# Four raw buffers for the first-layer expert weights, asked for four groups ahead

## What is computed

```python
def _moe_forward(x, router_w, router_b, w1, b1, w2, b2, top_k=2):
    logits = einsum('bsd,de->bse', x, router_w) + router_b
    top_vals, top_idx = top_k(logits, 2)
    keep = one_hot(top_idx, E).sum(-2) > 0
    gating = softmax(where(keep, logits, -1e30))
    h = relu(einsum('td,edh->eth', xf, w1) + b1[:, None, :])   # w1: 8 x 512 x 2048
    y = einsum('eth,ehd->etd', h, w2) + b2[:, None, :]         # w2: 8 x 2048 x 512
    out = einsum('etd,te->td', y, gf)
```

## Time and profile before

| | us |
|---|---|
| median of 3 runs | 1210.54 (1209.79 to 1211.63) |
| the profiled execution | 1207.57 |
| its span | 1205.8 |
| busy in the span: PE / DVE / ACT / POOL | 1102.9 / 926.9 / 694.9 / 474.2 |

### The profile page before, as it was taken

The page is one execution under the profiler, slowest core; times in us unless marked ns, Lnnn a source line. Parts: engine busy times, 40 slices in busy tenths (PEclk is TensorE's granted clock), DMA queues, the critical chain, the costliest instruction groups (busy, mean ns, idle before and its releaser), DMA issues.

```text
span 1205.8 us, 22592 instructions
## 1 busy us (share of the span) xinstructions
PE 1102.9 (91%) x7196; PEld 1014.9 (84%) x7197; DVE 926.9 (77%) x2049; ACT 694.9 (58%) x1387; POOL 474.2 (39%) x416
## 2 busy tenths in 40 slices
PE   4899999999999999999999999767887999788995
PEld 4799999999999999999999999644666987667895
DVE  6578888988888888889888888876776565876554
ACT  3456566565565665655656656441566665655654
POOL 6355656656556556556556552000121011121011
PEclk9899999999999999999999999975999999899998
DMA  5221121121221221211211210422777656776663
GB/s 182 96 73 57 47 71 42 59 71 39 62 71 39 62 59 50 62 52 58 62 51 59 62 42 2 152 105 59 256 244 233 206 173 231 233 247 193 199 191 96
DMA packets 78320, 131.11 MB, mean 109 GB/s; under 512 B 11336, under 2 KB 36040, under 8 KB 78288
## 3 DMA queue, kind: packets, MB, share of 16 engines
q1 hardware_dynamic: 74272, 120.73, 30.9%
q0 software_dynamic: 4016, 9.96, 3.7%
HBM read 123.34 MB, written 7.34 MB: 108 GB/s over the span
## 4 chain that ended last, share of the span: by engine, by line
PE 74%; DVE 11%; issue 5%; ACT 4%; DMA 3%; DVEq 1%; POOL 0%; ACTq 0%; SPq 0%; POOLq 0%
PE ps L421 17%; PE ps L423 16%; PE ps L422 16%; PE ps L1372 7%; PE ps L1424 7%; PE ps L1408 4%; PE ps L1409 3%; DMA w_raw<-in_w_dram 2%; DVE w_lo L1081 2%; DVE w_lo L1089 2%; DVE mx L1017 1%; DVE k_mix L939 1%; DVE pt_mix L1031 1%; ACT probs L749 1%; PE ps L1384 1%
## 5 line engine op out<-in xcount | busy, mean ns | idle before, releaser
L562 POOL TENSOR_TENSOR ctx_hi<-ctx_raw,no_query 128x1152 fp32r<-128x1152 f32 x64 | 143.0, 2234 | 290.5 <-PE ps L423 281.5
L939 DVE SCALAR_TENSOR_TENSOR k_mix<-ps,bk_sb,k_mix 64x384 fp32r<-64x384 f32 (+1 forms) x256 | 162.3, 634 | 82.2 <-ACT k_mix L709 77.9
L749 ACT ACTIVATE probs<-ps,negmax 128x1152 f32<-128x1152 f32 x64 | 78.3, 1223 | 200.9 <-DVE negmax L1020 200.9
L421 PE MATMUL ps<-wv_hi,ctx_hi 128*128 128x256 f32 (+1 forms) x624 | 181.9, 291 | 6.7 <-DVE k_mix L939 6.5
L566 POOL TENSOR_TENSOR ctx_lo<-ctx_raw,ctx_hi 128x1152 fp32r<-128x1152 f32 x64 | 179.7, 2807 | 5.0
L423 PE MATMUL ps<-wv_hi,ctx_lo 128*128 128x256 f32 (+1 forms) x624 | 175.8, 282 | 0.0
L422 PE MATMUL ps<-wv_lo,ctx_hi 128*128 128x256 f32 (+1 forms) x624 | 175.0, 280 | 0.0
L709 ACT ACTIVATE k_mix<-ps,bk_sb 64x384 fp32r<-64x384 f32 (+1 forms) x256 | 150.8, 589 | 24.1 <-PE ps L423 19.6
L1031 DVE TENSOR_TENSOR pt_mix<-ps,pt_mix 128x384 fp32r<-128x384 f32 (+1 forms) x256 | 142.1, 579 | 1.4 <-ACT pt_mix L760 1.4
L421 PE MATMUL ps<-ctx_hi,wk_hi 128*128 128x384 f32 (+1 forms) x384 | 133.4, 347 | 0.0
L423 PE MATMUL ps<-ctx_hi,wk_lo 128*128 128x384 f32 (+1 forms) x384 | 132.3, 345 | 0.0
(11 more groups left out here) (216 smaller groups left out, 2565.4 us busy)
## 6 DMA issues: line engine op xcount, KB each, us to landing
w_raw<-in_w_dram SPq DMA_DIRECT2D x68, 1024.0 KB, 6.8
ctx_raw<-in_ctx_t_dram SPq DMA_DIRECT2D x48, 576.0 KB, 3.8
ctx_raw<-in_ctx_t_dram SPq DMA_DIRECT2D x16, 673.5 KB, 4.0
q_both<-q_scratch SPq DMA_DIRECT2D x14, 128.0 KB, 3.0
x<-in_x_dram SPq DMA_DIRECT2D x1, 1024.0 KB, 5.5
wq_raw<-in_wq_dram SPq DMA_DIRECT2D x1, 1024.0 KB, 7.8
q_scratch<-q_out SPq DMA_DIRECT2D x1, 1024.0 KB, 5.8
wo_raw<-in_wo_dram SPq DMA_DIRECT2D x1, 1024.0 KB, 5.1
```

What stands on the lines that cost most here:

```text
L421: pe.matmul(acc_ap, a_hi, b_hi, start=start, stop=False)
L562: nc.gpsimd.tensor_tensor(ctx_hi[slot][:, :, 0:n], ctx_raw[slot][:, :, 0:n], no_query[:].rearrange("p (o i) -> p o i", o=1).broadcast_to([ ...
L939: last = nc.vector.scalar_tensor_tensor(out=k_mix[other, 2 * a + i, cols], in0=ps[rows, bank, 0:m], scalar=bk_sb[rows, a:a + 1], in1=k_mix ...
```

## The change

w1's raw pieces get two more buffers, `w1_more`, in the region that the output projection's weights leave (12 rows of 512 values; 8 of them are taken). The helper `w1_raw(group)` names the buffer of a group modulo 4, and each buffer has its own semaphore. Ahead of the loop, SP waits until the output projection has been multiplied (`x1_product`), then loads w1 of groups 2 and 3 of expert 0, and only then waits for the normalised rows and stores them. In the loop, at the place where SP loaded w1 of group `g + 2`, it now loads w1 of group `g` of the next block. The high and low parts keep two slots, and w2 keeps its two raw slots and its place in the order. At the end POOL waits for four w1 semaphores. Two more 1 MB loads are made in all.

```diff
+        w1_more = place("w1_more", [P, HG - 2, 4, BANK], F32, moe)
-        place("stage2_rest", [P, 3 * KD - BT, D], F32, moe)
+        place("stage2_rest", [P, 3 * KD - BT - 4 * (HG - 2), D], F32, moe)
-        w1_loaded = [sem(f"w1_loaded{i}") for i in range(2)]
+        w1_loaded = [sem(f"w1_loaded{i}") for i in range(HG)]
+        def w1_raw(group):
+            slot = group % HG
+            return w_raw[slot][:, 0] if slot < 2 else w1_more[:, slot - 2]
...
-                sp.dma_start(w_raw[slot][:, 0], src).then_inc(w1_loaded[slot], 16)
+                sp.dma_start(w1_raw(g), src).then_inc(w1_loaded[g], 16)
...
+            sp.wait_ge(x1_product, TT)
+            for g in range(2, HG):
+                load_w1(0, g)
             sp.wait_ge(xn_ready, 2 * TT)
...
                     sp.wait_ge(w1_split, pieces_done(b, g, PIECES - 1))
-                    load_w1(owner_next, (g + 2) % HG, g % 2)
+                    load_w1(expert_next, g)
                     sp.wait_ge(w2_split, pieces_done(b, g, PIECES - 1))
                     load_w2(owner_next, (g + 2) % HG, g % 2)
...
-                    act.wait_ge(w1_loaded[slot], 16 * (HG // 2 * b + group // 2 + 1))
-                nc.scalar.copy(w_hi[slot][:, 0, piece_of(piece), :], w_raw[slot][:, 0, piece_of(piece), :]
+                    act.wait_ge(w1_loaded[group % HG], 16 * (b + group // HG + 1))
+                nc.scalar.copy(w_hi[slot][:, 0, piece_of(piece), :], w1_raw(group)[:, piece_of(piece), :]
```

More of the change, by code:

```diff
@@ L493, in _, with load_w1 @@
             w2_view = w2.rearrange("e (g j p) d -> e g p j d", p=P, j=4)
-            def load_w1(e, g, slot):
+            def load_w1(e, g):
                 cols = slice(g * BANK, (g + 1) * BANK)
@@ L504, in load_w2 @@
                 sp.dma_start(w_raw[slot][:, 1], src).then_inc(w2_loaded[slot], 16)
-            load_w1(0, 0, 0)
+            load_w1(0, 0)
             load_w2(0, 0, 0)
             sp.wait_ge(pv_taken, STEPS * B + 1)
-            load_w1(0, 1, 1)
+            load_w1(0, 1)
             load_w2(0, 1, 1)
+            sp.wait_ge(x1_product, TT)
+            for g in range(2, HG):
+                load_w1(0, g)
             sp.wait_ge(xn_ready, 2 * TT)
@@ L678, in _ @@
             for i in range(2):
-                pool.wait_ge(w1_loaded[i], 16 * (HG // 2 * blocks + 1))
                 pool.wait_ge(w2_loaded[i], 16 * (HG // 2 * blocks + 1))
+            for i in range(HG):
+                pool.wait_ge(w1_loaded[i], 16 * (blocks + 1))
             pool.wait_ge(rows_moved, all_moved)
@@ L1080, in w1_low_piece @@
                 dve.wait_ge(w1_high, pieces_done(b, group, piece))
-                nc.vector.tensor_tensor(w_lo[slot][:, 0, piece_of(piece), :], w_raw[slot][:, 0, piece_of(piece), :],
+                nc.vector.tensor_tensor(w_lo[slot][:, 0, piece_of(piece), :], w1_raw(group)[:, piece_of(piece), :],
                                         w_hi[slot][:, 0, piece_of(piece), :].bitcast(F32),
```

## The result

| | before | after |
|---|---|---|
| median, us | 1210.16 (1207.86 to 1211.63, 4 runs) | 1194.62 (1192.12 to 1195.65, 4 runs) |
| ratio, 95% interval | | 0.9866 [0.9844, 0.9889] |
| the profiled execution / its span | 1207.57 / 1205.8 | 1195.65 / 1193.9 |

A forecast was written before the change was run, and what follows sets the result against it. VectorE was taken to carry the narrow blocks, idling behind ScalarE's wait for late w1. Removing that gives 14.7 us, less 2.0 for TensorE's clock: 12.7 us off the 1210.5 us median, 1197.8 us, range 1193.5 to 1203.

The forecast's parts named there:

- The late w1 and its price: Narrow blocks, groups 2 and 3: VectorE's idling behind ScalarE's wait for w1 goes, a gain of 14.7 us.
- w2 does not take its place: Narrow blocks: tightest w2 lands in about 5 us, under the 9.4 us limit, no cost; rival 1204.2 us, chance 0.07.
- The additions ahead of the loop: Two more w1 loads after the output projection cost nothing; rival of a late store, about 1213 us at worst, chance 0.04.
- What carries the block then: Narrow block after the change: VectorE stays the longest at 6.4 us per group, 0.3 us over TensorE.
- The DMA share of a narrow block: Same loads in 33 to 34 us instead of 37.9: the share goes from 0.77 to about 0.87.
- The clock: TensorE at block changes: half-speed falls cost 3.7 us, less 1.7 lost today, so 2.0 us to pay.
- the forecast's own range: Total time 1195.5 to 1200 us, for 0 to 3.5 clock falls, chance 0.70.
- the clock comes back: Rival: no block change is followed by a TensorE clock fall, 16.4 us gained, 1194.1 us; chance 0.08.
- no fall: Lower bound of the clock term at block changes: without any fall TensorE gives back 1.7 us.
- half-speed stretches at the starts of blocks: Sign of being right: after the change TensorE's half-speed stretches stand at block starts.
- the wide range: Total time 1193.5 to 1203 us, taking in both clock cases and leaving out the last three rivals.
- The rule on oscillation: Trainium skill: TensorE's clock stays up once waits for transfers are gone, turning the 2.0 us cost into 1.7 us gained.

The follow-up runs named there:

- two-ahead kernel: Changed kernel with its four buffers, but w1 asked for two groups ahead again and no extra loads ahead of the loop: 1210.69 us, ratio 1.0001.
- e_after_again: The changed kernel itself, unaltered, measured on another occasion: 1193.20 us, ratio 0.9875.
- w2 second in the queue: Changed kernel with both waits of a group first, then both loads, w1 ahead of w2: 1193.49 us, ratio 0.9879.
- three ahead: Changed kernel with w1 asked for three groups ahead and one load less ahead of the loop: 1196.13 us, ratio 0.988.
- no w1 loads: Changed kernel without any w1 load in the block loop, all blocks using the first expert's w1: 1193.77 us, ratio 0.9865.
- wide order: Changed kernel; at wide blocks' ends ScalarE and VectorE take gathered rows and gating ahead of the last w1 piece: 1195.68 us, ratio 0.9902.
- loads at the loop: Changed kernel with the two extra w1 loads made right ahead of the block loop, not after the output projection: 1197.55 us, ratio 0.9889.
- filling the pauses: Changed kernel with 9 unused TensorE products ahead of a narrow block's last output products and 14 behind them: 1194.76 us, ratio 0.9867.

## Why the prediction was right, point by point

**The late w1 and its price.** Right. The waits for w1 went from 33.3 us to none, and the gain was not 33.3 but what VectorE had idled. By narrow block the prediction's working gives 3.4, 3.8, 4.0 and 3.4 us, 14.7 in all; measured are 36.83 - 33.47 = 3.4, 37.88 - 34.84 = 3.0, 37.52 - 33.40 = 4.1 and 37.63 - 34.08 = 3.6 us, 14.1 in all. The longest landing of a w1 load is 12.4 us now, still far inside the 20 us of cover. That it is the asking and not the buffers is shown by the two-ahead kernel, and that nothing of w1 is left to gain by the one without its traffic.

**w2 does not take its place.** Right, with the size of its slack: no wait for w2 after. In the second profile of the changed kernel (`e_after_again`) w2 lands 5.3 us behind its request in the median and 5.9 at most, where the prediction took about 5; and with w2 second in the queue VectorE begins to wait just where the working had the limit.

**The additions ahead of the loop.** Right: no wait for the store, and POOL's gather still waits for VectorE's indices alone.

```profile
833.88 1.25 POOL L656 DMA_INDIRECT xg_raw<-xn_scratch,idx_next  x1 [32.64 <-DVE gate_next L1174]
```

**What carries the block then.** Right with a small gap. VectorE carries it, by 0.3 us per group over TensorE. When TensorE falls to half clock just then, this is not enough: at 899.0 the output products of group 1 take 4.5 us (898.65 to 903.11) instead of 2.86, and VectorE waits the 0.47 us seen above. Another 0.2 lie in VectorE's small instructions ahead of the selection, 0.70 us from 894.90 where they took 0.48, right behind the landing of the scatter at 894.3. These are most of the 0.8 us missing in the second block. In three of the kernels above (three ahead, no w1 loads, wide order) this block has neither, and takes 34.06 to 34.09 us, the 37.88 - 3.8 of the working. The DMA share of a narrow block, forecast at 0.87, came to 0.77 to 0.83. The half-speed stretches of the changed kernel, as stretches with the columns as above:

```profile
878.60:882.00 3.40, 3.24 (x8) 1.97 (x6) 3.35 (x4) 0.04 (x1) 0.00 (x0) 0.51 0.98 363
899.04:902.45 3.41, 3.41 (x10) 2.64 (x9) 3.41 (x4) 0.36 (x1) 2.51 (x2) 0.50 1.05 402
1045.80:1049.20 3.40, 3.40 (x9) 2.64 (x9) 3.40 (x4) 0.36 (x1) 0.00 (x0) 0.50 1.02 380
1079.95:1083.35 3.40, 3.40 (x9) 2.65 (x8) 3.40 (x4) 0.27 (x1) 0.00 (x0) 0.50 1.03 398
```

**The clock.** The term that was mis-sized, and its sign was wrong. The prediction charged 3.7 us for falls at block changes, less 1.7 for the one of before. In the changed kernel's profile no block change is followed by a fall (the first block begins at half clock, as before). Three of the four stretches lie in the last output products of a narrow block, beside VectorE busy for 3.35 to 3.40 of 3.40 us: they are hidden and cost nothing. The fourth is a part of the 0.8 us above. The third wide block, which had begun at half clock, takes 49.9 us instead of 51.05: that fall had cost 1.1 us, not 1.7. So the clock gave at least 1.1 - 0.8 = 0.3 us where -2.0 was forecast, and these 2.3 us are the larger part of the 3.2 between 1197.8 and 1194.6. The loop's 15.4 is 14.1 in the narrow blocks, 1.1 in the third wide one and 0.2 in the rest.

What failed was to expect falls behind the pauses at block changes, at the rate of the pauses in groups 2 and 3. Three rows of TensorE in the changed kernel, with the pause ahead in brackets:

```profile
877.31 0.50 PE L427 MATMUL ps<-w_hi,h_hi 128*128 128x512 f32 x1 [2.08 <-DVE h_lo L1308]
898.65 0.52 PE L427 MATMUL ps<-w_hi,h_hi 128*128 128x512 f32 x1 [0.81 <-DVE h_lo L1308]
917.78 0.39 PE L427 MATMUL ps<-xg_hi,w_hi 128*128 128x256 f32 x1 [2.62 <-DVE xg_lo L1189]
```

In three narrow blocks the fall came behind the 2.1 us ahead of the last output products, as at 877.31. It made these products longer, so the pause behind them was 1.0 to 1.1 us where 2.7 was forecast. In the second narrow block the pause at the change was the forecast one, 2.62 us, and no fall followed; the fall of this block had come behind 0.81 us. So the length of a pause alone does not tell whether a fall follows it. What does is left open.

The second profile of the changed kernel (`e_after_again`) has its four stretches in the same four places, and again a loop of 337.3 us. In kernels that differ from it by little some stand at block starts, and their loops take 340.8 us (three ahead) and 343.7 (loads at the loop). So this term can come out several microseconds apart between kernels that are nearly alike, by the small change or by chance, and one trace of the kernel before doesn't forecast it to a microsecond.

**The number.** 1194.6 lies outside the forecast's own range of 1195.5 to 1200, which was given a chance of 0.70, and 0.5 us from the rival *the clock comes back* (1194.1, chance 0.08). That rival's condition came true, no fall behind a block change; its reason did not, as four stretches are left. The forecast's own range was said to begin at no fall, for which the prediction's sum gives 1194.1 and not 1195.5. And one of its signs of being right, half-speed stretches at the starts of blocks, did not come. What the prediction had right is the late w1, 14.1 of 14.7 us; that the total lies in the wide range is owed to this range taking in both cases of the clock.

**The rule on oscillation.** By the Trainium skill (TensorE: Matmul & The Clock Gate, HAM oscillation) the clock would come back with the waits for transfers. The traces agree in the sum more than the prediction did (0.3 us gained), but not in the stretches: there were six between 870 and 1100 us and there are still four, three behind waits for VectorE of 2.1 us and one behind a wait of 0.81.

## What to carry to other kernels

A wait for a transfer is worth what the engine that carries the stage idles behind it, not its own length: 33.3 us here were worth 14.1, and 11.3 us elsewhere a few tenths. If a load is late, ask for it one step earlier; here one step, three groups ahead, was enough. The next load in the queue gets a deadline of its own, worked out for the shortened stage. Before moving work at the end of a stage, look for a transfer whose landing is waited for and whose start does not move with the work, here a scatter with 0.6 us to spare.

## What the hardware showed that was not expected

- A half-speed stretch of 3.4 us in TensorE's last products cost nothing in the three narrow blocks that ended with one, since VectorE was busy beside it; filling the pauses, which removed every such stretch, changed the four narrow blocks by 0.3 us in all.
- With half of the weight traffic gone (DMA share from about 0.8 to 0.5) no block changed by more than 0.8 us, and in the two that did (the second narrow and the second wide one) the half-speed stretches lie differently in the two traces.
- The same traffic does slow a scatter with addition. The sixteen scatters of 128 rows in the loop land behind their issue as below, first in the changed kernel, then without the w1 loads. In the narrow blocks of the changed kernel it is 7.3 to 9.7 us, where a 1 MB load of weights has a median of 6.8.

```profile
DMA to landing us min/median/max: 4.8/7.6/9.7
...
DMA to landing us min/median/max: 4.7/5.1/5.7
```
